# Quantisers without limiting operations in the preparation of quantised attention

## The reference, cut to what matters

```python
def _fq_sym(x, axis):                      # q, k: over the 16 numbers of a head; v: over all tokens
    s = jnp.max(jnp.abs(x), axis=axis, keepdims=True) / 127.0
    s = jnp.maximum(s, 1e-08)
    q = jnp.clip(jnp.round(x / s), -127.0, 127.0) * s
    return x + jax.lax.stop_gradient(q - x)

def weight_scale(W):
    return jax.lax.stop_gradient(jnp.max(jnp.abs(W))) / 7
W1_q = fake_quant(W1, sw1, -8, 7)          # clip(round(W1 / sw1), -8, 7) * sw1; the same for W2
```

## Time and profile before

| | |
|---|---|
| median of 3 runs | 2342.11 us (2340.34 to 2347.32) |
| the profiled execution's own time | 2353.1 us |
| its span, from first to last instruction | 2351.3 us |
| mean granted clock of TensorE | 0.797 of full speed |
| busy share of the span | PE 82%, PEld 47%, DVE 71%, ACT 57%, POOL 38% |
| the preparation | 1282.4 to 1399 us of the span |

### The profile page before, as it was taken

One profiled execution on the slowest core, in us unless ns is written; L12 is line 12 of the kernel. 1 busy time (PEld: TensorE's weight loads), 2 busy tenths in 40 slices (PEclk: granted clock), 3 DMA queues, 4 the chain that ended last, 5 costly groups with the idle time before them and its releaser, 6 DMA issues. The chain is left out here.

```text
span 2351.3 us, 49116 instructions
## 1 busy us (share of the span) xinstructions
PE 1924.7 (82%) x17689; PEld 1096.5 (47%) x17713; DVE 1659.9 (71%) x2791; ACT 1344.0 (57%) x1832; POOL 895.7 (38%) x778
## 2 busy tenths in 40 slices
PE   3776999999997885899987867888888888558855
PEld 1344656556564564478864432333333333334523
DVE  4776755555555557843335889999999999467975
ACT  3454633333334675543322349999999999545565
POOL 4750000000001461600023437888888888333301
PEclk9877999999997897999998675555555555588989
DMA  6343221122123105422322106656665566220110
GB/s 207 90 164 132 67 67 67 65 68 67 64 68 122 53 3 207 146 41 66 70 60 84 45 5 113 110 113 112 112 112 111 113 113 109 36 72 2 20 21 28
DMA packets 384868, 195.32 MB, mean 83 GB/s; under 512 B 312301, under 2 KB 355311, under 8 KB 382703
## 3 DMA queue, kind: packets, MB, share of 16 engines
q1 hardware_dynamic: 381617, 184.47, 32.4%
q0 software_dynamic: 3072, 8.39, 1.1%
HBM read 94.99 MB, written 23.09 MB: 50 GB/s over the span
## 5 line engine op out<-in xcount | busy, mean ns | idle before, releaser
L2465 POOL CAST qa_pT<-qa_eT 128x2048 bf16<-128x2048 uint8 x256 | 477.9, 1896 | 110.1 <-PE qa_OY L2491 94.5
L2578 ACT ACTIVATE qa_e<-qa_scores,qa_nb 128x2048 uint8<-128x2048 f32 x256 | 510.4, 1994 | 4.2
L2588 DVE TENSOR_SCALAR_CACHE_REDUCE qa_scores<-qa_S,qa_sq 128x1024 f32<-128x1024 f32 (+1 forms) x256 | 453.1, 1807 | 4.3 <-PE qa_S L2483 3.4
L2483 PE MATMUL qa_S<-qa_kT,qa_qT 32*128 32x512 f16 x1024 | 373.3, 615 | 95.6 <-DVE qa_scores L2588 94.3
L1116 POOL MEMSET rms_nothing<- 128x512 f16 x1 | 0.5, 525 | 579.9 <-POOLq L3496 579.9
L2483 PEld LDWEIGHTS qa_S<-qa_kT,qa_qT 32*128 32x128 f16 x1024 | 64.7, 108 | 310.1 <-DVE qa_scores L2588 266.9
L973 PE MATMUL moe_G<-hT,moe_W 128*128 (+1 forms) x792 | 193.8, 381 | 7.1 <-DVE moe_zero L941 7.1
L982 PE MATMUL moe_O<-moe_W,moe_ap 128*128 (+1 forms) x1584 | 194.6, 273 | 4.1 <-DVE moe_ap L937 4.1
L913 ACT ACTIVATE moe_ap<-moe_a 128x512 f16<-128x512 f32 x132 | 83.1, 629 | 195.5 <-DVE moe_a L935 195.5
L973 PE MATMUL moe_U<-hT,moe_W 128*128 (+1 forms) x792 | 192.7, 379 | 0.0
L982 PEld LDWEIGHTS moe_O<-moe_W,moe_ap 128*128 128x128 f16 x1584 | 154.6, 98 | 50.5 <-DVE moe_ap L937 3.9
(11 more groups left out here) (440 smaller groups left out, 3526.3 us busy)
## 6 DMA issues: line engine op xcount, KB each, us to landing
moe_wb<-weights_T SPq DMA_DIRECT2D x264, 128.0 KB, 2.8
moe_W<-in_moe_w SPq DMA_DIRECT2D x40, 384.0 KB, 11.4
moe_W<-in_moe_w SPq DMA_DIRECT2D x11, 1152.0 KB, 14.6
moe_xs_rows<-rms_nothing SPq DMA_DIRECT2D x46, 128.0 KB, 1.9
moe_ys_rows<-moe_ys SPq DMA_DIRECT2D x23, 256.0 KB, 2.1
conv_rows<-conv_parts SPq DMA_DIRECT2D x16, 256.0 KB, 3.2
qa_eT<-qa_e SPq DMA_TRANSPOSE x256, 3.1
conv_qst<-conv_rows SPq DMA_DIRECT2D x96, 32.0 KB
```

The costliest lines, as they stand in the source:

```text
L2465: nc.gpsimd.tensor_copy(pT[:, u % RING, :, :].rearrange("p (b r) q -> p b r q", r=2), pairs).then_inc(s_cast, 1)
L2483: last = nc.tensor.matmul(S[:, banks[i], :], qT[rows, g, t * P:(t + 1) * P], kT[rows, g, parts[i] * QW:(parts[i] + 1) * QW], start=True, s ...
L2578: nc.scalar.activation(e8[:, u % RING, :], scores[:, u % RING, :], ACT.Exp, bias=nb[:, p % 2, i:i + 1], accum_out=sums[:, u:u + 1]).then_i ...
L2588: nc.vector.tensor_scalar(target, S[:, banks[0]:banks[-1] + 1, :], sq[:, t, h:h + 1], so_far, ALU.mult, ALU.max, accum_out=greatest).then_ ...
```

## The change

The operations that limit the quotient go, and what is left of a quantiser is rounded by as few instructions as it needs.

```diff
     def integers(self, dve, i):                       # feed-forward weights, i = 0, 1
         f, w = (self.f1, self.f2)[i], (self.w1, self.w2)[i]
-        self.nc.vector.tensor_scalar(w[:, :], f[:, :], -8.0, None, ALU.max).then_inc(self.s_w, 1)
+        self.nc.vector.tensor_scalar(w[:, :], f[:, :], MAGIC, None, ALU.subtract).then_inc(self.s_w, 1)
-    def rounded(self, dve, i):
-        f = (self.f1, self.f2)[i]
-        self.chained(self.nc.vector.tensor_scalar(f[:, :], f[:, :], MAGIC, 7.0, ALU.subtract, ALU.min))
...
     def keys(p):
         chained(nc.vector.tensor_scalar(z, z, MAGIC, MAGIC, ALU.add, ALU.subtract))
-        chained(nc.vector.tensor_scalar(z, z, 127.0, -127.0, ALU.min, ALU.max))
...
     def queries(p):
-        chained(nc.vector.tensor_scalar(z, z, MAGIC, MAGIC, ALU.add, ALU.subtract))
         dve.wait_ge(s_Tk, p + 1)
-        nc.vector.tensor_scalar(slots(p, 0), by_head(z), 127.0, -127.0, ALU.min, ALU.max).then_inc(s_qi, 1)
+        nc.vector.tensor_scalar(slots(p, 0), by_head(z), MAGIC, MAGIC, ALU.add, ALU.subtract).then_inc(s_qi, 1)
...
     def value_integers():
-        chained(nc.vector.tensor_scalar(vT[:, :, :], vT[:, :, :], MAGIC, 127.0, ALU.subtract, ALU.min))
-        nc.vector.tensor_scalar(ints[:, :, :], vT[:, :, :], -127.0, None, ALU.max).then_inc(s_vi, 1)
+        nc.vector.tensor_scalar(ints[:, :, :], vT[:, :, :], MAGIC, None, ALU.subtract).then_inc(s_vi, 1)
...
     next_weights.divided(dve, 0)
-    next_weights.rounded(dve, 0)
     low(5)
     next_weights.integers(dve, 0)
...
     for p in range(PAIRS):
         queries(p)
         if p == 3:
             next_weights.divided(dve, 1)
-        if p == 4:
-            next_weights.rounded(dve, 1)
         if p == 5:
             next_weights.integers(dve, 1)
```

## The result

The changed kernel takes 2333.43 us in the median of 7 runs (2331.26 to 2336.68), the kernel before 2341.92 (2336.02 to 2347.32). The medians lie 8.5 us apart. The ratio on record is not that of the medians: it is 0.9957, 95% interval 0.9940 to 0.9974, which is 10.1 us less, 6.1 to 14.1. The forecast was 2333.8, 8.3 us less.

What follows compares the result with a forecast made beforehand. VectorE was taken to bound the attention loop and most of the preparation, with TensorE setting the keys. 0.47 + 1.26 + 2.73 = 4.46, plus 3.8 for queries, gave 8.3 us off 2342.1: 2333.8 us, 8-in-10 range 2329.5 to 2341.5.

Steps and rivals of the forecast that it cites:

- 0.47 us: Keys: of eight removed VectorE instructions only one shortens the stretch, 0.47 us, as TensorE's projections set pair 7's start.
- rival C: Keys: TensorE's clock is already high there, VectorE bounds, up to 3.3 us more come off, 2330.5 us; chance 0.05.
- the other 3.3 us: Keys: the rest of the removed VectorE time, beside TensorE's projections, becomes waiting.
- First weights, 1.26 forecast: First weight matrix: one removed instruction saves 1.26 us, all on VectorE's chain.
- bounded it there: Values: GpSimd's bias additions may shift the surviving integer instruction by one GpSimd instruction, 0.73 us either way.
- Value integers, 2.73 forecast: Value integers: one removed instruction saves 2.73 us, and the whole 4.46 us so far reaches the turned values.
- Queries, 3.8 forecast: Queries 2 to 7 with second weights: 20.84 us becomes 17.0, saving 3.8; queries 0 and 1 only add waiting.
- the 1 us that I had set aside: Queries: about 1 us unknown for when TensorE's clock rises.
- A: Queries: TensorE's clock stays at 0.50, 4.7 us a pair, giving back 5.1 us, 2342.7 us; chance 0.17.
- B: Pause before turned values: clock does not fall, queries 2 begin 2.1 us sooner, 10.4 us saved, 2331.7; chance 0.13.
- D: Values and turned tokens: clock stays at 0.50 through the queries, 10.5 us slower, 2352.6 us; chance 0.05.
- signs of being wrong: Keys shortened over 1 us, clock 0.50 through most queries, no low clock after pause, over 3 us change outside preparation.

Runs made afterwards that it cites:

- before_warm: Kernel before with 18 unread TensorE matmuls put ahead of key projection 2; ratio to the kernel before 1.0003 (0.9983 to 1.0022).
- after_warm: Changed kernel with 18 unread TensorE matmuls put ahead of key projection 2; ratio to the kernel before 0.9956 (0.9937 to 0.9975).
- after_filled: Changed kernel with unread matmuls in all TensorE's pauses, 8 of them ahead of the turned values; ratio to the kernel before 0.9962 (0.9947 to 0.9977).
- second pair of profiles: Kernel before and changed kernel run once more without edits; ratios to the kernel before 0.9997 and 0.9953.
- all_but_keys: Changed kernel with the keys' limiting instruction put back; ratio to the kernel before 0.9960 (0.9945 to 0.9974).
- keys_only: Kernel before with only the keys' limiting instruction removed; ratio to the kernel before 0.9990 (0.9976 to 1.0003).
- queries_only: Kernel before with only the queries' second instruction removed; ratio to the kernel before 1.0006 (0.9987 to 1.0024).
- after_no_bias: Changed kernel without GpSimd's 16 output bias additions, which changes the output; value stretch 9.66 us against 10.91.
- reordered: Changed kernel with VectorE doing queries 0 and 1 before the value integers, TensorE projecting queries 2 and 3 before the turned values; ratio to before 0.9964.
- reordered_filled: The reordered kernel with unread matmuls in TensorE's pauses and queries 4 projected between turned values 5 and 6; 2327.04 us, ratio to the kernel before 0.9945.
- before_filled: Kernel before with unread matmuls in all TensorE's pauses, 22 of them ahead of the turned values; ratio to the kernel before 0.9988 (0.9972 to 1.0004).

## Why the prediction was right

**The total.** 8.3 us forecast, 10.1 measured (6.1 to 14.1), the changed kernel's median 0.4 us from the forecast. By the sum of the profiled stretches it was 11.35: the keys gave 3.3 us more than forecast and the first weights 1.0 more, the queries 0.8 less. The interval holds 8.3 and 11.35 alike, so that the median fell so near the forecast is luck. What was right is where the gain comes from: VectorE's chain, with only its wait for queries 2 taking some of it.

**Keys, mis-sized.** I took TensorE at 1.2 GHz as given and had 0.47 us. Where TensorE keeps ahead, all eight count: 3.70 (`before_warm` against `after_warm`). The changed kernel was near that in 2 of 2 profiles (26.62 both; the clock rose on the way), so rival C, to which I gave 0.05, is what the profile shows. The first mistake was this chance. I read one execution's clock as the kernel's own, and my sentence that "nothing in the change speeds TensorE there, so it would be chance" made that chance small without a reason.

The second mistake lies in the 0.47 itself, which no run shows. I asked only when pair 7's keys come, and not what `low(0)` waits for behind them: ScalarE's copy of the first turned tokens, which follows TensorE. In the kernel before, ScalarE and VectorE:

```profile
1332.06 0.57 ACT L2239 ACTIVATE hT<-qa_hT_TP 128x512 f16<-128x512 f32 x1
...
1332.67 0.69 DVE L2303 TENSOR_TENSOR hT<-qa_hT_TP,hT 128x512 f16<-128x512 f32 x1
```

The copy ended at 1332.63, only 0.04 us ahead of `low(0)`. With TensorE unmoved, my estimate from these rows is now 0.04 us and not 0.47. `after_filled` has 0.45 (29.93), but in another way, as VectorE's timeline shows:

```profile
1302.35 1.09 DVE L2318 TENSOR_SCALAR qa_sk<-qa_sk 128x32 f32<-128x32 f32 x1
...
1309.33 0.69 DVE L2317 TENSOR_REDUCE qa_sk<-qa_QP 128x32 f32<-128x512 f32 x1 [0.47 <-PE qa_QP L2121]
...
1314.07 0.69 DVE L2312 TENSOR_TENSOR hT<-qa_hT_TP,hT 128x512 f16<-128x512 f32 x1 [0.97 <-ACT hT L2248]
```

`low(0)` waits 0.97 us for the turned tokens. The stretch is shorter because the clock was still high when key projection 2 began, so that TensorE began the last pair 21.23 us after VectorE's first key instead of 21.97. Nor did the other 3.3 us all become waiting for projections: these waits are 0.52, 0.13 and 0.47 us, and GpSimd's hold on L2318 (0.70, 1.09 and 0.74 us instead of 0.18) takes 2.0 more.

**First weights, 1.26 forecast, 2.22 measured.** 1.26 is the instruction; of the other 0.96, the output bias steps that escape GpSimd are 0.91 + 0.70 + 0.70 less 0.34 + 0.29 + 0.77, which is 0.91. The second pair of profiles has 1.75 and the pair with fill ahead of the keys 1.93, so 0.5 to 1.0 us came on top. I looked for GpSimd's hold on the values and bounded it there, but did not ask which instructions would leave its stretch. `all_but_keys` has it too (16.55).

**Value integers, 2.73 forecast and measured,** with 10.90 or 10.91 in every kernel with the edit and GpSimd's bias under the values as before. Without the edit it is 13.63 or 13.64, but 12.82 and 13.23 in `keys_only` and `queries_only`, whose low stretch is longer by 0.3 to 1.0: GpSimd started 7.15 and 7.40 us after the weights' maximum there instead of 7.55, so its hold falls on other instructions. The two stretches together are 32.2 to 32.6 without the edits and 27.1 to 27.7 with them. The surviving instruction kept its 2.70 us under GpSimd. All of it reached queries 2 (9.14 both). ScalarE's turned keys were nearly as late as the integers; its timeline of the changed kernel:

```profile
1335.56 9.97 ACT L2242 ACTIVATE qa_kT<-qa_TR 128x512 f16<-128x512 f16 x16 [4.17 <-PE qa_TR L2162]
```

They ended at 1345.53, only 0.1 us ahead of the integers instead of 1.4: 0.91 of that is VectorE's gain at the output bias steps, 0.35 ScalarE's, whose copies came that much later behind the slower TensorE. `after_no_bias` shows them overtaking.

**Queries, 3.8 forecast,** 2.96 in the first pair of profiles, 4.18 in the second, 4.80 in the pair with fill ahead of the keys, 3.83 with the clock held high. The difference is the clock's rise: in the profile after, queries 3 came 0.98 us late instead of 0.2, inside the 1 us that I had set aside.

**The rivals.** A did not decide, but its pace is real (4.7 us a pair in `reordered`). B did not come: the clock fell even earlier than before, during the turned keys. D was not seen. For B the Trainium skill's rule on long pauses (TensorE: Matmul & The Clock Gate, "HAM oscillation — how this bites in real kernels") is not what decided: in the profile after, the clock fell at about 1339.5 us where TensorE's waits were 1.1 us and shorter, with no long pause.

Of my signs of being wrong two came. The keys' stretch shortened by over 1 us, and in the first pair of profiles 11.1 us went ahead of the preparation. The second is not the change's: with the same code there, the kernel before starts the preparation at 1282 and 1288 us, with fill in all pauses at 1268.

**What stays open.** Without fill, the clock rose within the keys in all five profiles of kernels whose key work is shorter (4.0, 7.7, 7.8, 13.6 and 21 us after key projection 2 began), and in none of the four with the old key work (24 to 25 us after it, behind the keys, with the values). Nine profiles are few, and up to its rise TensorE kept the same 3.85 us a pair in all five as in the other four. The kernels with fill break the pattern both ways. `after_filled` and `reordered_filled`, with the shorter key work, stayed at 0.50 for 23.9 us, to the end of the key projections and beyond. `before_filled`, with the old key work, fell to 0.50 and rose again 14.8 us after key projection 2 began, among the keys (busy time, columns as in the earlier trace rows):

```profile
1295.50:1305.60 10.10, 9.58 (x41) 4.25 (x40) 9.51 (x21) 0.00 (x0) 5.29 (x6) 0.50 0.01 2
1305.70:1312.00 6.30, 5.47 (x39) 3.15 (x39) 5.96 (x13) 0.00 (x0) 3.40 (x4) 1.00 0.00 0
```

So, with fill ahead of them at least, a rise among the keys neither needs the shorter key work nor follows from it. Whether the change makes it likelier is not shown, and I have no cause to name. It also stays open how often the keys cost 26 and how often 30 us in executions that no profile saw.

## What to carry to other kernels

Where one engine alone is full, a removed instruction counts whole; where a second engine is nearly as slow, first ask at which clock that engine ran in the profile and price both cases with real chances. Then ask what the instruction behind the stretch waits for, since that may be due at the same moment. One execution's clock is a sample: 2 to 4 us of this kernel's 2340 hang on it in a single stage. And an engine that runs ahead of a neighbour with which it excludes itself changes which of its instructions pay for it: list those that leave the neighbour's stretch as well as those that enter.

## What the runs showed of the hardware that I had not expected

VectorE and GpSimd hold each other up even for tiny instructions: a 128x32 `tensor_scalar` of 0.18 us took 1.04 us, ending with GpSimd's 1.16 us instruction. The Trainium skill (SBUF — State Buffer, "Who interferes with whom") has whichever of the two begins first keep the ports that they share for its whole instruction, while the other stands. The row agrees, and so does `after_no_bias`: 3.18 to 2.48, 2.70 to 2.29 and 1.54 to 0.61 us with GpSimd's work gone.

TensorE can be busy for over 20 us without its clock rising: 22.98 of 26 us at 0.50 in the earlier trace rows, 23.78 of 24 in `after_filled`, both in the key projections; in `after_no_bias` the same projections had it high 4.0 us after key projection 2 began. The Trainium skill's account of the gate (TensorE: Matmul & The Clock Gate, "What's actually happening") has sustained activity release it; these rows differ from that, and the measurement decides.
